# Split products read and written from the last column to the first, and two pads in the second attention's memory

## The chip, the cores and the metric

The kernel runs on one core of a Trainium2 chip. The number that counts is the time of the whole program on the device, in microseconds. The engines are named as in the profile: PE is TensorE's matmul side, PEld its loading of weights, DVE is VectorE, ACT ScalarE, POOL GpSimd, SP the engine that issues the DMAs.

## What is computed

Two layers on 16 sequences of 64 tokens with 512 features each (1024 tokens), all in float32. `ctx` has the same shape as `x`.

```python
x = x + L0_xattn(layernorm(x), ctx)      # 32 query heads, 8 key heads, head size 128, rope, mask
x = x + L0_ffn(layernorm(x))             # silu(gate) * up, cut to whole numbers, 512 -> 1376 -> 512
x = x + L1_xattn(layernorm(x), ctx)      # keys and values from ctx and x joined, q and k rms-normalised
x = x + L1_ffn(layernorm(x))             # two 512 x 512 layers, fake int8 quantisation, gelu between them
```

Each attention projects queries (512 to 4096), keys and values (512 to 1024 each), and its output (4096 to 512). These projections, and the gate and up products of the first feed-forward, need more precision than one pass of TensorE's fast float32 form (`F32R`) has.

## The kernel before

**Split products.** Every operand of a projection is kept as two tiles, `hi` (the value rounded to `F32R`) and `lo` (what the rounding left). `split_product` (L63) makes from each pair of blocks three matmuls: hi by hi, lo by hi, hi by lo, and adds all of them up in one bank of PSUM. Its `lhs` is the stationary operand (the weights of the array, 128 x 128), its `rhs` the moving one. Each of the three has its own stationary block, so each matmul comes with its own weight load (PEld). All matmuls at L70 of the profile are those of `split_product`.

**Where it is called.** In `attention` three parts call it. `kv_job` holds a block of 128 tokens (`kv_hi`, `kv_lo`) still and streams 2 x 128 columns of the key and value weights. `q_job` holds 128 columns of the query weights still and streams 512 tokens of `kv_hi`, `kv_lo`. `project` holds 128 tokens of the attention's result (`o_hi`, `o_lo`) still and streams 512 columns of the output weights. In `int_ffn` the gate and up products hold 128 weight columns still and stream 512 tokens. The down product of `int_ffn` (L1774) is a loop of its own: 128 tokens of `hid` held still, `down_hi` and then `down_lo` streamed, 512 columns each.

**Order on PE.** The program of PE is written out by hand: in each of the 32 units of an attention it issues the scores of one unit, fills in with the projections of others (`filling`), turns the probabilities and weighs the values, and DVE, ACT and POOL take results out of PSUM, split them and prepare what comes next behind semaphores. Four PSUM banks (`proj`) rotate under the projections.

**Where the tiles lie.** Tiles are placed one behind the other in a partition's memory, from the left in the order of their allocation, or from the right for those with `side="right"`. Nearly all large tiles are a whole number of 512 bytes per partition, so two of them have the same rest by 512 bytes unless small tiles lie between them. In the first attention and the first feed-forward nothing small lies between `kv0_hi` and `kv0_lo`, the weights, and `o_hi` and `o_lo` or `hid`: all have one rest. In the second attention the weights `att1_w_hi` and `att1_w_lo` have that rest too, then come the small tiles of the last feed-forward (3 x 32, 64, 4 x 32 and 3 x 64 bytes, 480 in all), and then `q_cols`, `k_cols`, `v_rows`, `k_rows`, `o_hi`, `o_lo` and the rest, 32 bytes short of it. `kv1_hi` and `kv1_lo` are placed from the right end, at a rest 64 bytes short of that of the weights. The tiles of the last feed-forward later lie on the memory of `kv1`.

Of the kernel before, what the change touches and what calls it, by code (L numbers as in the profile page):

```python
# [5 lines left out]
F32 = mybir.dt.float32  # L6
# [7 lines left out]
P = 128  # L14
# [46 lines left out]
    pass  # L61


def split_product(eng, out, terms, first=True, last=True):


    n = 0
    for lhs_hi, lhs_lo, rhs_hi, rhs_lo in terms:
        for a, b in ((lhs_hi, rhs_hi), (lhs_lo, rhs_hi), (lhs_hi, rhs_lo)):
            ins = eng.matmul(out, a, b, start=(first and n == 0), stop=(last and n == 3 * len(terms) - 1))  # L70
            n += 1
    return ins

# [417 lines left out]
def attention(nc, st, tag, rope, weights, source=None, following=None, tail=None):  # L491
# [45 lines left out]
    for u in range(UNITS):  # L537
        g, n = divmod(u, 4)
# [24 lines left out]
    with ExitStack() as ctx:  # L563
        def sb(name, shape, dt=F32):
            return ctx.enter_context(nc.sbuf_tensor(f"{tag}_{name}", shape, dt))

        def sem(name):
            return st.sem(f"{tag}_{name}")

        q_cols = sb("q_cols", [P, 4, NBH, 2, S])  # L570
        k_cols = sb("k_cols", [P, NB * KL])
        v_rows = sb("v_rows", [P, NB * KL // P, HD])
# [993 lines left out]
def int_ffn(nc, st, tag, weights, following):  # L1566
# [3 lines left out]
    with ExitStack() as ctx:  # L1570
        def sb(name, shape, dt=F32):
            return ctx.enter_context(nc.sbuf_tensor(f"{tag}_{name}", shape, dt))

        hid = sb("hid", [P, CF, TOK], F32R)
# [26 lines left out]
        def x_cols(tile, k, h):  # L1601
            return tile[:, k, BANK * h:BANK * (h + 1)]

        def out_bank(t):

            return banks[(t + 4) % 8]

        def width(c):
            return P if c < WIDE else REST
# [17 lines left out]
        @block.sync  # L1627
        def _(eng):
            def load_next(c, m):
                for i in range(3):  # L1630
                    split.need(eng, c, i + 1)
                    weights.load(eng, i, c + 1, m)

            load_ctx(eng, st, st.spare, 0)
            following.load(eng, 3)
            with eng.Fori(0, WIDE - 1) as c:
                load_next(c, P)
            load_next(WIDE - 1, REST)
            split.need(eng, 0, 3 * CF)
            for n in range(3):  # L1640
                following.load(eng, n)
# [105 lines left out]
        @block.tensor  # L1747
        def _(eng):
            pair_full.start(eng)

            def body(c, sub, m, m_next):
                split.need(eng, c, 2)
                for h in range(HALF):
                    if isinstance(c, int) and c == 0 and h == 1:
                        for t in range(4, NT):
                            intake.turn(eng, t)
                        eng.wait_ge(intake.x_split, 4)
                    pair_drained.need(eng, c, h + 1 - PAIRS)
                    for i in range(2):
                        last = split_product(eng, banks[4 * sub + 2 * h + i][:m], [  # L1760
                            (gu_hi[:, sub, i, k, 0:m], gu_lo[:, sub, i, k, 0:m],
                             x_cols(x_hi, k, h), x_cols(x_lo, k, h))
                            for k in range(KT)])
                    last.then_inc(pair_full.sem, 1)

            chunk_passes(eng, body)
            split.need(eng, 0, 3 * CF)
            for t in range(NT):
                if t % (NT // HALF) == 0:
                    clipped.need(eng, 0, CF * HALF - 1 + t // (NT // HALF))  # L1770
                for c in range(CF):
                    m = width(c)
                    for i, down in enumerate((down_hi, down_lo)):
                        last = eng.matmul(out_bank(t)[:], hid[:m, c, t * P:(t + 1) * P], down[:m, c, :],  # L1774
                                          start=(c == 0 and i == 0), stop=(c == CF - 1 and i == 1))
                last.then_inc(out_full, 1)

# [4 lines left out]
def build(nc, a, out):  # L1782
    st = State()
    with ExitStack() as ctx:
        st.sem = lambda name: ctx.enter_context(nc.semaphore(name))

        def sb(name, shape, dt=F32):
            return ctx.enter_context(nc.sbuf_tensor(name, shape, dt))
# [13 lines left out]
        def columns_scope(tag, n, side="left"):  # L1802

            scope = ExitStack()
            st.kv_hi, st.kv_lo = (scope.enter_context(nc.sbuf_tensor(f"{tag}_{part}", [P, KT, n], F32R, side=side))
                                  for part in ("hi", "lo"))
            return scope

        first = AttentionWeights(st, "att0", a["wq0"], a["wk0"], a["wv0"], a["wo0"])
# [12 lines left out]
                int_ffn(nc, st, "ffn0", inner, second)  # L1822
        with ExitStack() as scope:
            second.place(nc, scope)
            columns_scope("kv1", 2 * TOK, side="right").close()
            ffn = QuantFfn(nc, st, scope, "ffn1", a["gamma"], a["beta"], a["w1"], a["b1"], a["w3"], a["b3"], out)
            attention(nc, st, "att1", False, second, tail=ffn)
# [42 lines left out]
```

## Time and profile before

| | us |
|---|---|
| median of 3 runs | 1535.55 |
| lowest, highest | 1535.22, 1535.87 |
| span of the profiled execution | 1536.3 |

The profiled execution is one run of the program; its span goes from the first instruction to the last. An engine's busy time is the time in which at least one of its instructions is open. Matmuls are pipelined: the duration of one is longer than the distance from its start to the start of the next, so a rate is read from start to start and not from durations. A row of the timeline gives the start of a group of equal instructions that follow each other, the time from the first one's start to the last one's end, and after `x` how many they are.

### The profile page before, as it was taken

The numbers are of one execution on the slowest core, as the hardware profiler recorded it, in microseconds if no ns is written. First come the engines' busy times: TensorE is split into PE (matmuls) and PEld (weight loads), VectorE is DVE, ScalarE is ACT, GpSimd is POOL, SyncE is SP. The second block draws the span as 40 slices with busy tenths as digits, with TensorE's granted clock in tenths as the row PEclk, the third lists the DMA queues.
The fourth block names the chain that finished last, engine by engine and source line by source line (L and its number), as shares of the span: only waits on it lengthen the run. The fifth ranks groups of instructions, "written<-read, shape, count | busy, mean of one in ns | idle before, by whom it ended". The sixth has DMA issues, their size and how long they took to land.

```text
span 1536.3 us, 28681 instructions
## 1 busy us (share of the span) xinstructions
PE 1481.3 (96%) x11533; PEld 1273.9 (83%) x11536; DVE 950.8 (62%) x1983; ACT 599.3 (39%) x1434; POOL 564.6 (37%) x468
## 2 busy tenths in 40 slices
PE   6899999999999998999899999999999999999985
PEld 5788888888888877887788899888889989888973
DVE  7656666665666575666866455555645645565588
ACT  4313222221222234442355354444435444443556
POOL 4535354443535414561233132222312222231248
PEclk9999999999999999999899999999999999999999
DMA  6101021111102003220112011011101111010201
GB/s 197 42 28 53 19 68 29 42 38 33 48 22 70 21 6 98 75 57 21 48 30 62 1 42 29 28 43 28 42 1 42 29 29 42 21 50 1 83 2 55
DMA packets 84302, 64.45 MB, mean 42 GB/s; under 512 B 7280, under 2 KB 71024, under 8 KB 84176
## 3 DMA queue, kind: packets, MB, share of 16 engines
q1 hardware_dynamic: 83600, 62.47, 14.1%
q8 instruction: 91, 1.49, 0.4%
q14 instruction: 35, 0.29, 0.1%
q10 hardware_dynamic: 576, 0.20, 0.1%
HBM read 60.56 MB, written 2.10 MB: 41 GB/s over the span
## 4 chain that ended last, share of the span: by engine, by line
PE 47%; DVE 2%; POOL 1%; issue 1%; ACT 0%; DVEq 0%; ACTq 0%; POOLq 0%
PE att_proj L70 35%; PE att_att L798 4%; PE att_sco L756 4%; PE att_att L773 2%; PE att_proj L720 1%; PE att_sco L735 1%; POOL ffn_y L476 0%; DVE ffn_top L428 0%; DVE ffn_y L470 0%; POOL x_rows L414 0%; DVE ffn_y L424 0%; PE att_att L242 0%; DVE stats L383 0%; DVE x_rows L1051 0%; ACT ffn_y L435 0%
## 5 line engine op out<-in xcount | busy, mean ns | idle before, releaser
L148 POOL TENSOR_TENSOR att_w_lo<-w_raw,att_w_hi 128x512 fp32r<-128x512 f32 x160 | 207.0, 1319 | 183.3 <-ACT att_w_hi L143 175.8
L1414 POOL TENSOR_TENSOR att_probs<-att_probs,att_total 128x512 f32<-128x512 f32 x64 | 82.9, 1295 | 458.5 <-DVE att_total L1035 344.5
L70 PE MATMUL att_proj<-att_w_hi,kv_hi 128*128 128x256 f32 x768 | 221.7, 289 | 9.7 <-DVE kv_lo L260 9.7
L70 PE MATMUL att_proj<-att_w_hi,kv_lo 128*128 128x256 f32 x768 | 216.5, 282 | 0.0
L70 PE MATMUL att_proj<-att_w_lo,kv_hi 128*128 128x256 f32 x768 | 216.4, 282 | 0.0
L70 PE MATMUL att_proj<-kv_hi,att_w_hi 128*128 128x512 f32 x512 | 208.7, 408 | 1.5 <-DVE kv_lo L251 1.5
L70 PE MATMUL att_proj<-att_w_hi,att_o_hi 128*128 128x512 f32 x512 | 207.0, 404 | 1.9 <-issue 1.9
L70 PE MATMUL att_proj<-kv_lo,att_w_hi 128*128 128x512 f32 x512 | 202.7, 396 | 0.0
L70 PE MATMUL att_proj<-kv_hi,att_w_lo 128*128 128x512 f32 x512 | 202.6, 396 | 0.0
L70 PE MATMUL att_proj<-att_w_lo,att_o_hi 128*128 128x512 f32 x512 | 201.5, 394 | 0.0
L1051 DVE TENSOR_TENSOR x_rows<-att_proj,x_rows 128x512 f32<-128x512 f32 x128 | 88.4, 691 | 182.4 <-PE att_proj L70 182.3
L70 PE MATMUL att_proj<-att_w_hi,att_o_lo 128*128 128x512 f32 x512 | 201.2, 393 | 0.0
L1261 ACT ACTIVATE att_probs_t<-att_att 128x512 f32<-128x512 f32 x96 | 54.1, 598 | 364.5 <-PE att_att L773 364.5
L70 PEld LDWEIGHTS att_proj<-att_w_hi,kv_hi 128*128 128x128 f32 x768 | 146.4, 191 | 12.0 <-issue 9.6
L70 PEld LDWEIGHTS att_proj<-att_w_lo,kv_hi 128*128 128x128 f32 x768 | 146.5, 191 | 0.0
L70 PEld LDWEIGHTS att_proj<-att_w_hi,kv_lo 128*128 128x128 f32 x768 | 146.4, 191 | 0.0
L1251 ACT ACTIVATE att_probs<-att_sco,att_low,att_q_rms 128x128 f32<-128x128 f32 x256 | 113.9, 464 | 57.2 <-DVE att_low L1015 57.2
L1400 POOL TENSOR_TENSOR att_q_cols<-spare 128x512 f32<-128x512 f32 x64 | 85.8, 1341 | 121.5 <-DVE spare L966 121.5
L70 PE MATMUL ffn_bank<-kv_hi,kv_lo 128*128 128x512 f32 (+1 forms) x528 | 121.8, 393 | 6.3 <-DVE kv_hi L251 4.6
L70 PEld LDWEIGHTS ffn_bank<-kv_hi,kv_lo 128*128 128x128 f32 (+1 forms) x528 | 98.7, 187 | 29.1 <-DVE kv_hi L251 4.9
L70 PEld LDWEIGHTS att_proj<-kv_lo,att_w_hi 128*128 128x128 f32 x512 | 97.1, 190 | 22.7
L70 PEld LDWEIGHTS att_proj<-att_w_hi,att_o_hi 128*128 128x128 f32 x512 | 96.4, 188 | 23.0 <-issue 2.1
(167 smaller groups left out, 2743.6 us busy)
## 6 DMA issues: line engine op xcount, KB each, us to landing
w_raw<-in_wq SPq DMA_DIRECT2D x64, 256.0 KB, 2.9
w_raw<-in_wo SPq DMA_DIRECT2D x64, 256.0 KB, 2.8
w_raw<-in_wk SPq DMA_DIRECT2D x16, 256.0 KB, 3.0
w_raw<-in_wv SPq DMA_DIRECT2D x16, 256.0 KB, 3.5
w_raw<-in_gate_t SPq DMA_DIRECT2D x10, 256.0 KB, 2.9
w_raw<-in_up_t SPq DMA_DIRECT2D x10, 256.0 KB, 3.2
w_raw<-in_down_t SPq DMA_DIRECT2D x10, 256.0 KB, 3.0
spare<-in_ctx_t SPq DMA_DIRECT2D x4, 512.0 KB, 5.2
```

The costliest lines, as they stand in the source:

```text
L70: ins = eng.matmul(out, a, b, start=(first and n == 0), stop=(last and n == 3 * len(terms) - 1))
L148: eng.tensor_tensor(self.lo[:, chunk], self.raw[:, n % RAW_SLOTS], raw(self.hi[:, chunk]), ALU.subtract)\
L720: last = eng.matmul(proj[job % 4][rows, b:b + 1], squares[:, u % 2, b, g, part], st.ones[:, 0:1], start=True, stop=True)
L735: last = eng.transpose(bank[:, c * P:(c + 1) * P], k_rows[:, 4 * i + c], st.ident[:])
L756: last = eng.matmul(sco[job % 2][:, cols], q_cols[:, u % 4, b, :, :], k_cols[:, key], start=True, stop=True)
L773: last = eng.transpose(bank[:, c * P:(c + 1) * P], flat[:, (4 * i + c) * P:(4 * i + c + 1) * P], st.ident[:])
L798: last = eng.matmul(att_bank("out", u, i)[:, cols], v_rows[:, NBH * h + 4 * i + c], probs_t[:, i, cols], start=True, stop=True)
L1051: eng.tensor_tensor(st.x[:, row], proj[job % 4][:], st.x[:, row], ALU.add).then_inc(proj_drained, 1)
L1251: ins = eng.activation(probs[:, u % 2, b], sco[(u * SJ + i) % 2][:, c * KL:(c + 1) * KL], ACT.Exp, bias=low[:, u % 2, one], scale=q_rms[:, ...
L1261: eng.activation(probs_t[:, slot], att_bank("turn", u, i)[:], ACT.Copy).then_inc(turned_copied, 1)
L1400: eng.tensor_tensor(dst, a, b, ALU.add).then_inc(rotated, 1)
L1414: eng.tensor_tensor(probs[:, u % 2, 0:n], probs[:, u % 2, 0:n], total[:, u % 2, 0:n].unsqueeze(2).broadcast_to([P, n, KL]), ALU.mult)\
```

## The change

`backward` reverses the order in which an access pattern goes through its free dimensions; the numbers it names stay the same. `split_product` and the down product apply it to the output and to the moving operand, so column 511 (or 255) is read and written first and column 0 last, and each result still lands at its old address. The stationary operand is named as before. Two tiles that nobody uses are added in the second attention: 32 bytes ahead of `q_cols`, and 448 bytes at the right end ahead of `kv1_hi`. With them all large tiles of the second attention, and those of the last feed-forward at the right end, have the rest by 512 bytes that the weights have.

```diff
+def backward(ap):
+
+    return ap[:, ::-1] if len(ap.shape) == 2 else ap[:, ::-1, ::-1]
+
+
 def split_product(eng, out, terms, first=True, last=True):
-
 
     n = 0
     for lhs_hi, lhs_lo, rhs_hi, rhs_lo in terms:
         for a, b in ((lhs_hi, rhs_hi), (lhs_lo, rhs_hi), (lhs_hi, rhs_lo)):
-            ins = eng.matmul(out, a, b, start=(first and n == 0), stop=(last and n == 3 * len(terms) - 1))
+            ins = eng.matmul(backward(out), a, backward(b), start=(first and n == 0),
+                             stop=(last and n == 3 * len(terms) - 1))
             n += 1
     return ins
 
@@ -567,6 +572,8 @@
         def sem(name):
             return st.sem(f"{tag}_{name}")
 
+        if not rope:
+            sb("pad", [P, 8])
         q_cols = sb("q_cols", [P, 4, NBH, 2, S])
         k_cols = sb("k_cols", [P, NB * KL])
         v_rows = sb("v_rows", [P, NB * KL // P, HD])
@@ -1771,7 +1778,7 @@
                 for c in range(CF):
                     m = width(c)
                     for i, down in enumerate((down_hi, down_lo)):
-                        last = eng.matmul(out_bank(t)[:], hid[:m, c, t * P:(t + 1) * P], down[:m, c, :],
+                        last = eng.matmul(backward(out_bank(t)[:]), hid[:m, c, t * P:(t + 1) * P], backward(down[:m, c, :]),
                                           start=(c == 0 and i == 0), stop=(c == CF - 1 and i == 1))
                 last.then_inc(out_full, 1)
 
@@ -1822,6 +1829,7 @@
                 int_ffn(nc, st, "ffn0", inner, second)
         with ExitStack() as scope:
             second.place(nc, scope)
+            scope.enter_context(nc.sbuf_tensor("kv1_pad", [P, 112], F32, side="right"))
             columns_scope("kv1", 2 * TOK, side="right").close()
             ffn = QuantFfn(nc, st, scope, "ffn1", a["gamma"], a["beta"], a["w1"], a["b1"], a["w3"], a["b3"], out)
             attention(nc, st, "att1", False, second, tail=ffn)
```

## Rows read from the trace of the kernel before

**Rows 1.** Page, part 1: busy us, share of the span and instructions by engine.

```profile
PE 1481.3 (96%) x11533; PEld 1273.9 (83%) x11536; DVE 950.8 (62%) x1983; ACT 599.3 (39%) x1434; POOL 564.6 (37%) x468
```

**Rows 2.** Page, part 4: the chain that ended last, by engine and line.

```profile
PE 47%; DVE 2%; POOL 1%; issue 1%; ACT 0%; DVEq 0%; ACTq 0%; POOLq 0%
```

**Rows 3.** Stages: length; PE, PEld, DVE, ACT, POOL busy; granted clock; DMA share; GB/s.

```profile
0.00:574.00 574.00, 553.60 (x4080) 470.89 (x4080) 371.78 (x657) 158.12 (x287) 255.95 (x223) 0.99 0.17 48
574.00:748.00 174.00, 165.94 (x720) 134.57 (x720) 110.69 (x190) 68.62 (x121) 68.28 (x53) 0.98 0.21 57
...
757.00:1450.00 693.00, 692.91 (x6308) 618.54 (x6307) 392.37 (x972) 318.59 (x912) 184.69 (x146) 1.00 0.11 30
```

**Rows 4.** Groups by line and form, two of nine like these: count, busy us, mean ns.

```profile
L70 PE MATMUL att_proj<-att_w_hi,kv_hi 128*128 128x256 f32 x768 | 221.7, 289 | 9.7 <-DVE kv_lo L260 9.7
...
L70 PE MATMUL att_proj<-kv_hi,att_w_hi 128*128 128x512 f32 x512 | 208.7, 408 | 1.5 <-DVE kv_lo L251 1.5
```

**Rows 5.** Timeline of PE, first attention, output products: first and last of 22.

```profile
310.21 0.39 PE L70 MATMUL att_proj<-att_w_lo,att_o_hi 128*128 128x512 f32 x1
...
314.97 0.39 PE L70 MATMUL att_proj<-att_w_lo,att_o_hi 128*128 128x512 f32 x1
```

**Rows 6.** Timeline of PE, first attention, query products: first and last of 12.

```profile
298.22 0.40 PE L70 MATMUL att_proj<-kv_hi,att_w_hi 128*128 128x512 f32 x1
...
300.74 0.39 PE L70 MATMUL att_proj<-kv_lo,att_w_hi 128*128 128x512 f32 x1
```

**Rows 7.** Timeline of PE, feed-forward: 57 gate and up products; down products, first and last of 38.

```profile
639.51 13.08 PE L70 MATMUL ffn_bank<-kv_hi,kv_lo 128*128 128x512 f32 x57
...
714.62 0.39 PE L1774 MATMUL ffn_bank<-ffn_down_hi,ffn_hid 128*128 128x512 f32 x1
...
723.12 0.40 PE L1774 MATMUL ffn_bank<-ffn_down_lo,ffn_hid 128*128 128x512 f32 x1
```

**Rows 8.** Timeline of PE, second attention: outputs, 1st and 23rd; queries, 1st and 12th.

```profile
1007.22 0.40 PE L70 MATMUL att_proj<-att_w_hi,att_o_lo 128*128 128x512 f32 x1
...
1012.36 0.40 PE L70 MATMUL att_proj<-att_w_lo,att_o_hi 128*128 128x512 f32 x1
1012.59 0.39 PE L70 MATMUL att_proj<-kv_hi,att_w_hi 128*128 128x512 f32 x1
...
1015.16 0.39 PE L70 MATMUL att_proj<-kv_lo,att_w_hi 128*128 128x512 f32 x1
```

**Rows 9.** Timeline of PE, keys and values: first attention, 1st and 43rd; second, 1st and 69th.

```profile
293.06 0.28 PE L70 MATMUL att_proj<-att_w_lo,kv_hi 128*128 128x256 f32 x1
...
298.10 0.28 PE L70 MATMUL att_proj<-att_w_lo,kv_hi 128*128 128x256 f32 x1
...
1026.64 0.28 PE L70 MATMUL att_proj<-att_w_hi,kv_hi 128*128 128x256 f32 x1
...
1034.65 0.28 PE L70 MATMUL att_proj<-att_w_lo,kv_hi 128*128 128x256 f32 x1
```

**Rows 10.** Timeline of PE: groups of bf16 products with 512 columns, and eight transposes.

```profile
1520.87 0.81 PE L461 MATMUL att_proj<-ffn_w_t,ffn_x_t 128*128 128x512 bf16 x3
...
1528.98 1.24 PE L461 MATMUL att_proj<-ffn_w_t,ffn_x_t 128*128 128x512 bf16 x5
...
1462.70 1.04 PE L773 MATMUL att_att<-ident,att_probs 128*128 128x128 f32 x8
```

**Rows 11.** Timeline of all engines near 310.4 us: a matmul, and the next one's weight load.

```profile
310.44 0.39 PE L70 MATMUL att_proj<-att_w_hi,att_o_hi 128*128 128x512 f32 x1
310.44 0.19 PEld L70 LDWEIGHTS att_proj<-att_w_hi,att_o_lo 128*128 128x128 f32 x1
```

**Rows 12.** Timeline of PE: split products, 1st and 7th; that stretch's windows row (columns as above).

```profile
1470.69 0.63 PE L70 MATMUL att_proj<-att_w_hi,att_o_lo 128*128 128x512 f32 x1
...
1473.25 0.62 PE L70 MATMUL att_proj<-att_w_hi,att_o_lo 128*128 128x512 f32 x1
...
1470.50:1473.60 3.10, 3.10 (x8) 2.42 (x8) 2.92 (x10) 0.00 (x0) 2.00 (x3) 0.50 0.03 5
```

## The prediction

> **What bounds the kernel now.** Begin with the busy times: PE is busy 96% of the span, DVE 62%, ACT and POOL under 40% [rows 1]. The chain that ended last is mostly PE too [rows 2]. Then the stages: in the second attention PE is busy for 692.91 of 693 us, in the first for 553.6 of 574, in the feed-forward for 165.9 of 174, and the next busiest engine, DVE, needs 392, 372 and 111 us there; the granted clock is 0.98 to 1.00, the upper level of 2.4 GHz [rows 3]. So what a product costs on PE goes into the time nearly one for one, and no engine is near to taking over.
>
> A busy PE is not PE at its peak, so read its rate next, from start to start. Split products with 512 moving columns (six groups of 512 in the attentions, 528 gate and up products, 176 down) and with 256 (three groups of 768) are 3776 and 2304 in number [rows 4]. The distance between them:
> - first attention, outputs: 314.97 - 310.21 over 21 steps, 0.2267 us [rows 5]; queries: 2.52 over 11, 0.2291 [rows 6]
> - feed-forward, gate and up: (13.08 - 0.39) over 56, 0.2266; down: 8.50 over 37, 0.2297 [rows 7]
> - second attention, outputs: 5.14 over 22, 0.2336; queries: 2.57 over 11, 0.2336 [rows 8]
> - keys and values: 5.04 over 42, 0.1200 in the first attention, 8.01 over 68, 0.1178 in the second [rows 9].
>
> Against that, bf16 products with 512 columns stand (1.24 - 0.81) over 2, 0.215 us apart, and eight transposes (1.04 - 0.27) over 7, 0.110 [rows 10]. The second number is the pace at which 128-column weight loads can follow each other. Every split product is thus 8 to 19 ns over what PE does elsewhere in this trace. At the lower clock level (granted 0.50) the same products stand 2.56 over 6, 0.4267 apart, less than twice 0.215: there the excess is gone [rows 12].
>
> **What the excess is.** Same instruction, same shape, same engine, yet the output products take 0.2267 where weights and `o_hi` have one rest by 512 bytes, and 0.2336 where the rests differ by 32 bytes [rows 5, 8]. Keys and values go the other way, 0.1200 with one rest and 0.1178 with two [rows 9]. So time depends on where the two operands lie: what I read from it is that a product's moving operand and the next product's weight load get into each other's way in memory. The two start within the same hundredth of a microsecond [rows 11]. A product reads 2048 bytes in 0.215 us, four turns of 512; a weight load reads 512 bytes in 0.110 us, one turn. If they collide whenever they are at the same place of a turn, and run in opposite senses, they meet 2 + 1 = 3 times in the 0.110 us that both read; in the same sense 2 - 1 = 1 time, and from the same start that one meeting falls on the very end. The excess of 11.7 ns (0.2267 - 0.215) would be 3.9 ns a meeting. No row shows in which sense weights are read; that they go from the last column to the first is an assumption of the forecast. The Trainium skill (TensorE: Matmul & The Clock Gate, section Weight-path perf modes) says of another mode that its first 128 weight columns are loaded reversed, and gives the chunks of the fast weight load a negative step; no run here shows it for float32.
>
> **Reversing the products.** It adds and removes no instruction, no wait and no byte, and the order on every queue stays. What is to be had, with 0.215 and 0.110 as floors, is number times excess:
> - outputs, first attention: 768 x 11.7 ns = 9.0 us; queries 768 x 14.1 = 10.8
> - gate and up: 528 x 11.6 = 6.1; down 176 x 14.7 = 2.6
> - second attention: outputs 768 x 18.6 = 14.3; queries 768 x 18.6 = 14.3
> - keys and values: 768 x 10.0 = 7.7 and 1536 x 7.8 = 12.0
>
> In all 76.8 us. That is the upper bound. What stays is between 0 and one meeting of 3.9 ns; I take 3 ns, near one meeting, since the two reads start together only to within a hundredth of a microsecond and a product that is a few columns ahead catches up just before the load ends. 6080 x 3 ns = 18.2 us. The gain is 76.8 - 18.2 = 58.6 us. The lower bound of the edit is a loss, and is priced below. It also reverses the order of writing into PSUM; no row shows a backward write, so its price lies between nothing and the half-pace case below, and I take nothing, as every product writes the same 2048 bytes of the same bank.
>
> **The pads.** They cost no time of any engine: 32 and 448 bytes of memory, nothing fills or reads them. They bring every pair of operands in the second attention to one rest, on which the sum above relies. By themselves, with products still forward, they would turn the second attention's rates into those of the first: outputs 768 x 6.9 ns = 5.3 us less, queries 768 x 4.5 = 3.5 less, keys and values 1536 x 2.2 = 3.4 more, 5.4 us less in all. The other matmuls there keep the rest between their own operands except the transposes against `ident`, which already run at 0.110.
>
> **What is late next.** If the second attention gets some 40 us shorter, PE has about 650 us of work against 392 on DVE; in the feed-forward about 158 against 111 [rows 3]. The waits of the others for PE shorten with it. The start and the last feed-forward have few split products and don't change.
>
> **The sum.** 1536.3 - 58.6 = 1477.7 us for an execution like the profiled one. Its span is 0.75 us above the median of 1535.55, so the median goes to 1477.
>
> **Rivals.**
> 1. *Direction does nothing, rests do.* The excess is there in both senses, and only the pads act: 1535.55 - 5.4 = 1530 us. For it: every observed difference is between rests, none between senses. Against it: meetings that depend on the place should depend on the sense. Between this and the forecast lies a partial gain.
> 2. *Nothing changes.* The excess belongs to the weight load as such, and rests that seem to matter are neighbours in the program. 1535.5 us. The Trainium skill holds this (TensorE: Matmul & The Clock Gate, section Part 2, on LDWEIGHTS: loading the next weights takes no read bandwidth from the running matmul; SBUF — State Buffer, section SBUF: two separate sides: PE never waits on anyone there). The trace disagrees: 0.2267 and 0.2336 for one form [rows 5, 8].
> 3. *The product is held behind the weight load.* In the same sense a single meeting can last. If the weight load has the lead when they start, the product can't pass and goes at the load's pace for 0.110 us: 128 columns instead of 256, so 128 columns late, 0.215 / 4 = 54 ns. 6080 x 54 ns = 328 us, less the 76.8 of present excess: 1535.55 + 251 = 1787 us. It decides on who is first inside the hundredth of a microsecond of [rows 11]: if the product is, it pulls away.
> 4. *A descending stream runs at half pace*, in reading or in writing PSUM, at about the distance seen at the low clock: 3776 x (0.427 - 0.230) + 2304 x (0.213 - 0.118) = 744 + 219 = 963 us more, about 2500. The Trainium skill (SBUF — State Buffer, the box on cachelines) says that a non-contiguous PSUM pattern slows matmuls much; whether descending counts as that no run here shows, and neighbours stay neighbours.
>
> **How the numbers follow.** Forecast, between the whole 76.8 and about half of it, 1458 to 1500 us: 0.60. Rival 1 and the partial gains above 1500: 0.20. Rival 2: 0.08. Rival 3: 0.07. Rival 4: 0.05. The number is the forecast's, 1477. The range takes in the first two, 1458 to 1531, and leaves out 0.20. A measurement of this kernel tells about 0.2% from no change, 3 us, so rival 1 still counts as faster: faster 0.80, within 0.2% 0.08, slower 0.12.
>
> **What would show it.** In the timeline of the changed kernel the output products of both attentions should stand 0.215 to 0.219 us apart, and keys and values 0.110 to 0.114, with no difference left between first and second attention. The counts, the stages outside the split products and the granted clock stay. If outputs stand 0.2267 apart in both, it is rival 1; if 0.27, rival 3; if 0.43 at a granted clock of 1.00, rival 4. The forecast is wrong in its root if weights are read from the first column to the last: then the present sense is already the good one, and reversal adds meetings.

## The result and the profile after

| | before | after |
|---|---|---|
| median, us | 1535.71 (4 runs) | 1548.84 (4 runs, 1545.52 to 1550.14) |
| span of the profiled execution | 1536.3 | 1548.2 |
| PE busy | 1481.3 | 1493.6 |

The changed kernel is slower: its ratio is 1.0082, with a 95% interval of 1.007 to 1.0094. The forecast was a gain of 58.6 us; a loss of 13 us was measured, on the other side of no change and outside the range. The page of the changed kernel, part 1, answers [rows 1]:

```profile
span 1548.2 us, 28684 instructions
PE 1493.6 (96%) x11536; PEld 1274.9 (82%) x11536; DVE 949.0 (61%) x1983; ACT 597.2 (39%) x1434; POOL 561.2 (36%) x468
```

Busy time rose on PE by 12.3 us and the span by 11.9; PEld gained 1.0, and the other three lost 2 to 3 each. The windows of the stages (columns as in [rows 3]) say where:

```profile
0.00:574.00 574.00, 554.32 (x4051) 466.22 (x4052) 365.07 (x648) 155.43 (x283) 254.35 (x223) 0.99 0.17 48
574.00:748.00 174.00, 166.29 (x714) 131.99 (x713) 109.23 (x184) 68.30 (x121) 67.60 (x53) 0.98 0.21 57
757.00:1450.00 693.00, 686.54 (x6241) 612.12 (x6242) 390.20 (x955) 317.52 (x911) 183.26 (x145) 0.99 0.11 32
```

PE is as busy as before and gets through fewer matmuls in the same 574 us: 4051 against 4080. The stage ends later, and the later stages start later; that the third window is a little less full comes from that shift, since the pause between the stages now lies in it (from 775 to 1450 PE is busy for 674.84 of 675 us, where it was 674.91). The granted clock is the same: 0.99 and 0.98 in the first two windows, and 1.00 from 775 on in both kernels. So the rate of the products has changed, and it is read from start to start, as in [rows 5 to 9]. The timeline of PE in the first attention, output products (1st and 21st of 21) and query products (1st and 12th of 12):

```profile
301.86 0.40 PE L74 MATMUL att_proj<-kv_hi,att_w_hi 128*128 128x512 f32 x1
...
304.43 0.40 PE L74 MATMUL att_proj<-kv_lo,att_w_hi 128*128 128x512 f32 x1
...
311.19 0.40 PE L74 MATMUL att_proj<-att_w_lo,att_o_hi 128*128 128x512 f32 x1
...
315.85 0.40 PE L74 MATMUL att_proj<-att_w_hi,att_o_lo 128*128 128x512 f32 x1
```

Outputs stand 4.66 over 20, 0.2330 us apart, where they were 0.2267 [rows 5]; queries 2.57 over 11, 0.2336, where they were 0.2291 [rows 6]. In the feed-forward, 87 gate and up products; then the second attention, outputs (1st and 27th) and keys and values (1st and 20th):

```profile
639.72 20.46 PE L74 MATMUL ffn_bank<-kv_hi,kv_lo 128*128 128x512 f32 x87
...
1017.14 0.40 PE L74 MATMUL att_proj<-att_w_hi,att_o_hi 128*128 128x512 f32 x1
...
1023.21 0.40 PE L74 MATMUL att_proj<-att_w_lo,att_o_hi 128*128 128x512 f32 x1
...
1033.73 0.28 PE L74 MATMUL att_proj<-att_w_lo,kv_hi 128*128 128x256 f32 x1
...
1035.98 0.28 PE L74 MATMUL att_proj<-att_w_hi,kv_hi 128*128 128x256 f32 x1
```

Gate and up: (20.46 - 0.40) over 86, 0.2333 (0.2266 in [rows 7]). Outputs: 6.07 over 26, 0.2335, as before [rows 8]. Keys and values: 2.25 over 19, 0.1184 (0.1178 in [rows 9]). In this kernel a backward product of 512 columns goes at one pace, about 0.2334, which is the slow pace of the kernel before; nothing came near 0.215.

The mean distance in nanoseconds over all pairs of neighbours in an unbroken stretch, by kind of product, for the two kernels and the variants of the next section:

| | keys/values, att 0 | queries | outputs | gate/up | down | keys/values, att 1 | queries | outputs |
|---|---|---|---|---|---|---|---|---|
| before | 119.7 | 229.7 | 227.6 | 227.1 | 229.5 | 117.6 | 233.0 | 233.0 |
| after | 118.4 | 233.6 | 233.4 | 233.3 | 233.9 | 118.3 | 233.8 | 233.5 |
| direction alone | 118.4 | 233.6 | 233.4 | 233.4 | 233.9 | 119.9 | 233.6 | 233.4 |
| pads alone | 119.6 | 229.8 | 227.6 | 227.0 | 229.2 | 119.9 | 228.2 | 227.5 |

Number times difference accounts for the loss: outputs of the first attention 768 x 5.8 ns = 4.5 us, queries 768 x 3.9 = 3.0, gate and up 528 x 6.2 = 3.3, down 176 x 4.4 = 0.8, outputs and queries of the second attention 768 x 1.3 = 1.0, keys and values 768 x 1.3 = 1.0 less in the first and 1536 x 0.7 = 1.1 more in the second. In all 12.7 us, against 11.9 in the spans.

### The profile page after: what moved, and what is told of

The parts are those of the page before. It is cut to its first block, busy times and chain, and to the rows that moved or that the text cites. A ratio compares the mean times of both kernels' runs of the same rounds, so it can differ in the third digit from the quotient of the medians.

```text
span 1548.2 us, 28684 instructions
## 1 busy us (share of the span) xinstructions
PE 1493.6 (96%) x11536; PEld 1274.9 (82%) x11536; DVE 949.0 (61%) x1983; ACT 597.2 (39%) x1434; POOL 561.2 (36%) x468
## 4 chain that ended last, share of the span: by engine, by line
PE 46%; DVE 3%; POOL 1%; issue 1%; ACT 0%; DVEq 0%; ACTq 0%; POOLq 0%
PE att_proj L74 34%; PE att_att L805 4%; PE att_sco L763 4%; PE att_att L780 2%; PE att_proj L727 1%; PE att_sco L742 1%; POOL ffn_y L481 0%; DVE ffn_top L433 0%; DVE ffn_y L475 0%; POOL x_rows L419 0%; DVE att_probs_t L232 0%; DVE ffn_y L429 0%; DVE stats L388 0%; DVE kv_lo L265 0%; PE att_att L247 0%
## 5 line engine op out<-in xcount | busy, mean ns | idle before, releaser
L74 PEld LDWEIGHTS att_proj<-att_w_hi,kv_hi 128*128 128x128 f32 x768 | 146.1, 190 | 13.2 <-issue 11.0
L74 PE MATMUL ffn_bank<-kv_hi,kv_lo 128*128 128x512 f32 (+1 forms) x528 | 126.1, 403 | 5.9 <-DVE kv_hi L256 4.1
```

The lines of the kernel that those rows point to most:

```text
L74: ins = eng.matmul(backward(out), a, backward(b), start=(first and n == 0), stop=(last and n == 3 * len(terms) - 1))
```

## Experiments in the whole kernel

**Direction alone.** The changed kernel without its pads.

```diff
-        if not rope:
-            sb("pad", [P, 8])
...
-            scope.enter_context(nc.sbuf_tensor("kv1_pad", [P, 112], F32, side="right"))
```

> The changed kernel without its two pads: products go from the last column to the first, the second attention's tiles keep the rests of before. After the change a product with 512 columns stands 0.2335 us from the next in every stage, where it was 0.227 to 0.230 in the first attention and the feed-forward and 0.233 in the second attention. Theory A (the reversal itself costs 6 ns a product wherever the rests were alike, and the pads do nothing for backward products): 1548 us, and 0.2335 in the second attention too. Theory B (backward products want unlike rests, and the pads spoil that): the second attention comes nearer to 0.215 and the whole is under 1535 us.

Measured: 1549.88 us against 1536.44 (ratio 1.0086, 1.0072 to 1.01). So the direction is the loss, all of it. With backward products the pads matter in one kind only, keys and values of the second attention, 119.9 without and 118.3 with: 1536 x 1.6 ns = 2.5 us, 2.0 between the profiled spans (1550.2 and 1548.2).

**Pads alone.** The kernel before with the two pads.

```diff
+        if not rope:
+            sb("pad", [P, 8])
...
+            scope.enter_context(nc.sbuf_tensor("kv1_pad", [P, 112], F32, side="right"))
```

> The kernel before with the two pads and nothing else: forward products, all rests alike. If forward products with one rest are the good case wherever they stand, the second attention's output products go from 0.2336 to 0.227, its queries to 0.229, its keys and values from 0.1178 to 0.120, and the time is 5 us shorter, 1530 us. If neighbours in the program and not the rests make the difference, 1535.5 us.

Measured: 1532.69 us against 1536.44, ratio 0.9975 (0.9966 to 0.9985), 3.8 us less. The timeline of PE in the second attention, outputs (1st and 22nd), then keys and values (1st and 22nd):

```profile
1006.05 0.39 PE L70 MATMUL att_proj<-att_w_lo,att_o_hi 128*128 128x512 f32 x1
...
1010.81 0.39 PE L70 MATMUL att_proj<-att_w_lo,att_o_hi 128*128 128x512 f32 x1
...
1024.89 0.28 PE L70 MATMUL att_proj<-att_w_lo,kv_hi 128*128 128x256 f32 x1
...
1027.40 0.28 PE L70 MATMUL att_proj<-att_w_lo,kv_hi 128*128 128x256 f32 x1
```

Outputs 4.76 over 21, 0.2267, against 0.2336 [rows 8]; keys and values 2.51 over 21, 0.1195, against 0.1178 [rows 9]. So the rest counts for forward products, with opposite signs here for 512 and for 256 columns. By the table the terms are 768 x 5.5 = 4.2 and 768 x 4.8 = 3.7 less, 1536 x 2.3 = 3.5 more: 4.4 us less, which is also the difference between the profiled spans (1536.3 and 1531.9).

**Which of the two reversals.** Each of these two kernels has one of them alone, in `split_product` and in the down product, so the results land mirrored in their rows:

```diff
-            ins = eng.matmul(backward(out), a, backward(b), ...
+            ins = eng.matmul(out, a, backward(b), ...            # moving operand alone
+            ins = eng.matmul(backward(out), a, b, ...            # output alone
```

> The changed kernel with the moving operand alone backward; the output is written forward, so the results land mirrored in their rows. The parts run gave 0.2334 for this at every rest. If reading is what costs: the same as the changed kernel, 1548 to 1549 us.

> The changed kernel with the output alone written backward, the moving operand read forward; the results land mirrored. The parts run gave 0.2277 for this at rest 0. If writing into PSUM backward costs nothing: the time of the pads alone, 1533 us.

Moving operand alone: 1549.77 us against 1536.05, ratio 1.0093 (1.0078 to 1.0108), with the rates of the changed kernel. Output alone: 1532.83, ratio 0.9977 (0.9968 to 0.9987), with the rates of pads alone. The first and the 21st output product of the first attention, output alone:

```profile
311.22 0.39 PE L74 MATMUL att_proj<-att_w_hi,att_o_hi 128*128 128x512 f32 x1
...
315.75 0.39 PE L74 MATMUL att_proj<-att_w_lo,att_o_hi 128*128 128x512 f32 x1
```

They are 4.53 over 20, 0.2265 apart. Writing PSUM from the last column to the first costs nothing; reading the moving operand that way is the whole price.

## Experiments on the product by itself

These kernels leave out the computation and issue blocks of 48 products on PE alone, 12 after each other into each of four PSUM banks. Unless said otherwise, each product has another stationary block than the one before, and the loops have the form

```python
for k in range(48):
    eng.matmul(o(k), still[:, 128*(k%32) : +128], moved[:, 512*(k%8) + d : +512], ...)   # [:, ::-1] for back
```

where 4 d is the rest, the bytes by which the moving operand lies past the stationary one by 256. A row holds a whole block, so the distance is (length - length of one) over 47, and one is 0.39 to 0.40 us long (0.28 with 256 columns, 0.38 with bf16). Each such run was made once. The first products of a block sometimes go at another pace, so a mean over 48 can stand 1 ns off the steady one.

**All rests, both directions.**

> Leaves out the whole computation: TensorE alone runs runs of 48 products of 128x128 by 512 columns in float32r, each with a stationary block of its own, one run for each distance of 0, 32, ... 480 bytes between the rests of moving and stationary operand, forward and backward; the other engines are idle. If moving operand and weight load meet in memory, the distance from start to start depends on the rest: forward, 0.227 at 0 and 0.233 at 32 and at 448; backward, somewhere in the scan it falls to 0.215 to 0.219. If the excess belongs to the weight load as such, it is 0.226 or more at every rest and in both directions.

The timeline of PE: forward at rests 0, 32, 64 and 256, back at 0 and 256.

```profile
44.10 11.04 PE L68 MATMUL bank<-moved,still 128*128 128x512 f32 x48
54.98 11.37 PE L70 MATMUL bank<-moved,still 128*128 128x512 f32 x48
66.19 11.16 PE L72 MATMUL bank<-moved,still 128*128 128x512 f32 x48
...
133.22 11.05 PE L84 MATMUL bank<-moved,still 128*128 128x512 f32 x48
...
222.34 11.37 PE L100 MATMUL bank<-moved,still 128*128 128x512 f32 x48
...
311.95 11.36 PE L116 MATMUL bank<-moved,still 128*128 128x512 f32 x48
```

Forward, rest 0 and rest 256 give (11.04 - 0.39) / 47 = 0.2266, rests 64 and 320 give 0.2291, all others 0.2331 to 0.2341. The pattern repeats after 256 bytes, not 512. Backward, all 16 rests give 0.2333 to 0.2335. The rates of both whole kernels are found again here without any other engine at work.

**The parts of it.**

> Leaves out the whole computation, as the scan of rests; runs of 48 products that tell apart what the reversal is made of: the moving operand alone backward, the output alone backward, 256 columns in both directions, rests in steps of 4 bytes, 128 columns, one and the same stationary block for all, and bf16. If reading is what costs, the moving operand alone backward takes 0.2335 at rest 0 and the output alone 0.227; if writing is, the other way round. If the weight load is the partner, bf16 products show 0.215 in both directions. 256 columns: 0.120 forward at rest 0, 0.118 backward.

Moving operand alone back (rest 0), output alone back (rest 0), 256 columns forward at 0 and at 192, 256 columns back at 0, and bf16 back:

```profile
43.85 11.37 PE L68 MATMUL bank<-moved,still 128*128 128x512 f32 x48
...
133.47 11.09 PE L84 MATMUL bank<-moved,still 128*128 128x512 f32 x48
...
222.02 5.91 PE L100 MATMUL bank<-moved,still 128*128 128x256 f32 x48
...
239.12 5.63 PE L106 MATMUL bank<-moved,still 128*128 128x256 f32 x48
...
267.16 5.84 PE L116 MATMUL bank<-moved,still 128*128 128x256 f32 x48
...
513.66 10.52 PE L170 MATMUL bank<-moved_b,still_b 128*128 128x512 bf16 x48
```

The moving operand is the slow part (0.2334) and the output is not: the block's mean is 0.2277, but only its first products are slower, and its second half stands at 0.2266, the forward pace. With 256 columns forward is 0.1198 at rest 0, the rest that all keys and values of the first attention have, and 0.1138 at 192; backward is 0.1183 at rest 0. Plain bf16 has no such excess in either direction: 0.2158 forward once steady, 0.2158 back. The same run has rests from 4 to 28 bytes, and there backward isn't one pace: the means are 0.2334 and 0.2336 at rests 28 and 16, 0.2355 to 0.2367 at 4, 8, 20 and 24, and 0.2399 at 12.

**Does the excess follow the weight load?** This is the test of the forecast's main step. If the products meet the loads, a stationary block of 32 columns, a quarter of the bytes, must show a quarter of the meetings.

> Leaves out the whole computation, as the scan of rests; runs of 48 float32r products. The stationary block has 128, 96, 64 or 32 columns, so that its load is shorter and the product of 512 columns is not. If the excess over 0.2155 is made of meetings of the product's reading with the next weight load (11 ns forward and 18 ns backward at rest 0 with 128), it shrinks with the block: at 32 columns to about a quarter, 3 and 4 ns. If it is a fixed price of float32r or of the direction, it stays at 11 and 18 whatever the block. Moving both operands on by the same bytes changes nothing if only the distance between them matters. Products of 384, 320 and 192 columns: the excess is that of 512, since the load is over in 0.11 us.

Stationary block of 128 columns, forward and back, then of 32 columns, forward and back, all at rest 0; then 128 columns forward with both operands moved on by 16 and by 32 bytes:

```profile
44.01 11.04 PE L68 MATMUL bank<-moved,still 128*128 128x512 f32 x48
...
88.45 11.36 PE L76 MATMUL bank<-moved,still 128*128 128x512 f32 x48
...
311.75 11.29 PE L116 MATMUL bank<-moved,still 128*32 128x512 f32 x48
...
356.25 11.36 PE L124 MATMUL bank<-moved,still 128*32 128x512 f32 x48
...
411.98 11.21 PE L134 MATMUL bank<-moved,still 128*128 128x512 f32 x48
...
423.03 11.09 PE L136 MATMUL bank<-moved,still 128*128 128x512 f32 x48
```

With 32 columns the forward excess is larger ((11.29 - 0.39) / 47 = 0.2319 against 0.2266), and backward the distance is 0.2334 with 128, 96, 64 and 32 columns alike. The loads did get shorter, from 188 to 109 ns in the mean. So the excess isn't a number of meetings that shrinks with the load. The stationary block still has some part in it forward, since its width changed the pace by 5 ns; what part, no run shows.

Moving both operands on by the same bytes keeps the distance between them. By 32, 64 and so on up to 224 bytes it changed nothing (0.2266 in the second half of each block), so what counts isn't the place of the moving operand by itself. But by 16, 48 and so on up to 240 bytes all eight blocks stood at 0.230. So the distance between the two isn't all that counts either, unless it is what the block before did, since blocks of both kinds ran in turn.

384 columns took 0.1734 forward and 0.1778 back at rest 0, 320 columns 0.147 at every rest and in both directions, 192 columns 0.111 to 0.112 likewise. At 192 columns that is about the 0.110 of the transposes [rows 10], so there the weight load is likely what sets the pace. With 320 columns the same loads follow each other at 0.147, so they don't set it, and direction and rest have dropped out all the same.

**What does the excess need?**

> Leaves out the whole computation, as the other runs of 48. Is the excess one of the number form or of the bytes that are read? bf16 with a step of 2 in the moving operand covers 2048 bytes per 512 columns as float32r does: theory of the bytes, its 0.2158 rises and depends on rest and sense; theory of the form, it stays 0.2158. float32r that reads one and the same column 512 times: theory of the bytes, no excess (0.2155) and no difference of senses; theory of the form, 0.2267 or more. Columns of 224 to 496: all distances so far settle near a whole multiple of 6.67 ns (113.3, 120, 226.7, 233.3, 240), 8 cycles of 1.2 GHz; if that is a grain, the distance goes in such steps and not with every 16 columns.

First bf16 with every second column read, so that 512 columns span 2048 bytes, forward and back (47 of 48 records); then float32 with one column read 512 times, output back (with the output forward only the first product was slower); then eight columns read 64 times:

```profile
44.16 10.78 PE L90 MATMUL bank<-moved_b,still_b 128*128 128x512 bf16 x47
54.78 11.26 PE L92 MATMUL bank<-moved_b,still_b 128*128 128x512 bf16 x47
...
229.76 10.52 PE L124 MATMUL bank<-moved,still 128*128 128x512 f32 x48
...
272.81 10.53 PE L132 MATMUL bank<-moved,still 128*128 128x512 f32 x48
```

Spread over 2048 bytes, bf16 has the excess too: (10.78 - 0.39) / 46 = 0.2259 forward, where the record that is missing is at an end of the block, and (11.26 - 0.39) / 47 = 0.2313 backward, where it is inside. Float32 that reads the same one or eight columns again has none: (10.52 - 0.38) / 47 = 0.2157. So it isn't the format. Nor is it the length of the weight load: bf16 products of 128 columns stand 0.056 apart where float32 ones stand 0.111, so bf16 loads take at most half the time, and spread bf16 has the excess all the same. It goes with the new bytes that the moving operand spans per column: it is there with 4 a column (float32, or bf16 with every second column) and not with 2 (plain bf16) or with columns that repeat. A stationary block of one repeated column leaves it, 0.2317 forward and 0.2333 back. By length it is no price per column. As a yardstick take the columns over the 2.4 GHz of the upper clock level, which is 213.3 ns for 512 and 106.7 for 256: at rest 0, 512 columns are 13.3 above it forward and 20 back, 256 columns 13.1 and 11.7, 448 columns (186.7) 16 and 20, 320 columns (133.3) 13.3 both ways. I had expected whole steps of 6.67 ns; 226.7, 233.3 and 240 do stand on such steps, 202.7 with 448 columns doesn't.

**Rest in steps of 4 bytes.**

> Leaves out the whole computation, as the scan of rests; forward products with 512 and with 256 columns at every rest from 0 to 252 bytes in steps of 4. The scan by 32 repeats after 256 bytes. If the meetings have a grain of some bytes there are narrow good rests that the steps of 32 and 64 bytes missed; for 512 columns better than 0.2267, for 256 better than the 0.1139 at 192. If 0 and 192 are already the best, the whole gain that placement can give in this kernel is that of the query, output and feed-forward products at 0 and of keys and values at 192.

Forward, 512 columns at rest 0 and 256 columns at rests 0, 16, 112 and 192:

```profile
42.99 11.04 PE L68 MATMUL bank<-moved,still 128*128 128x512 f32 x48
...
761.19 5.91 PE L196 MATMUL bank<-moved,still 128*128 128x256 f32 x48
...
784.06 5.60 PE L204 MATMUL bank<-moved,still 128*128 128x256 f32 x48
...
921.13 5.64 PE L252 MATMUL bank<-moved,still 128*128 128x256 f32 x48
...
1035.84 5.62 PE L292 MATMUL bank<-moved,still 128*128 128x256 f32 x48
```

For 512 columns rest 0 is the best of 64 (0.2266); the worst, 20, 116 and 212, have 0.240. For 256 columns rest 0 is in the middle of the 64 (0.1198), 16, 112 and 192 are the best (0.1132 to 0.1140), and the worst, 4, has 0.1230. This points to a kernel with two rests. It also tells when the direction matters: forward is under 0.2330 at 28 of the 64 rests and near or above backward's 0.2333 at the other 36, so a product on a poor rest has little to lose by reversal. In the kernel before, those of the second attention had such a rest.

## From the findings to a faster kernel

**Keys and values at rest 192.** The kernel before with two pads (the one ahead of `kv1_hi` is 128 bytes here), and a gap of 64 bytes inside each weight tile behind the two chunks that hold key and value weights, the tile moved on so that these lie at 192 and the query and output weights at 0:

```diff
+class Chunks:
+    SHIFT = 16
...
+        self.head = tile[:, 0:n].rearrange("p (c n) -> p c n", n=BANK)
+        self.rest = tile[:, n + self.SHIFT:CHUNKS * BANK + self.SHIFT].rearrange("p (c n) -> p c n", n=BANK)
...
+        if ahead:
+            tile("w_ahead", ahead, F32)
```

> Forward products and the two pads, and in both attentions the key and value weights moved so that they lie 192 bytes (by 256) past the tokens they are multiplied with, while query, output and feed-forward products stay at a rest of 0. The fine scan gives 0.1137 us for 256 columns at 192 and 0.1200 at 0. Theory of the map (each product costs what the scan shows for its own rest and sense): 2304 products x 6.3 ns = 14.5 us off the 1532.7 of the pads alone, 1518 us, a ratio of 0.988 to the kernel before. If another engine or the queues behind the products hold it, less than half of that.

Measured: 1524.46 us against 1536.05, ratio 0.992 (0.9906 to 0.9935). It falls 6 us short of what was expected, and the rows name the place of most of it: keys and values of the first attention (1st and 45th), and two stretches of those of the second (22 and 70 products):

```profile
292.06 0.28 PE L70 MATMUL att_proj<-att_w_hi,kv_hi 128*128 128x256 f32 x1
...
297.25 0.28 PE L70 MATMUL att_proj<-att_w_lo,kv_hi 128*128 128x256 f32 x1
...
1017.02 0.28 PE L70 MATMUL att_proj<-att_w_lo,kv_hi 128*128 128x256 f32 x1
...
1019.41 0.28 PE L70 MATMUL att_proj<-att_w_lo,kv_hi 128*128 128x256 f32 x1
...
1020.59 0.28 PE L70 MATMUL att_proj<-att_w_lo,kv_hi 128*128 128x256 f32 x1
...
1028.72 0.28 PE L70 MATMUL att_proj<-att_w_lo,kv_hi 128*128 128x256 f32 x1
```

5.19 over 44, 0.1180; 2.39 over 21, 0.1138; 8.13 over 69, 0.1178. The same instructions on tiles with the same rests have two steady paces, even a microsecond apart. The mean over all was 117.7 in the first attention and 114.2 in the second. Against the 113.7 that was expected this is 768 x 4.0 = 3.1 us and 1536 x 0.5 = 0.8; where the other 2 to 3 us are isn't shown.

**Is it the place or the predecessor?** The tiles at the addresses of each attention, and then blocks of keys behind blocks of queries and the other way round.

> Leaves out the whole computation: key and query products alone, with the blocks, the order hi, lo, hi and the distances between tiles that the first and the second attention have, other engines idle, the weights moved on by 0 to 240 bytes in steps of 16. In the kernel with keys at 192 the second attention's keys and values stand 0.1142 us apart as the scan says, the first attention's 0.1177 instead of 0.1137. If the layout of the first attention makes that, it shows here too, 0.1177 at 192 in the first layout and 0.1137 in the second, and another rest may be better for it; if the work of the other engines makes it, both layouts show 0.1137 here. Queries: 0.2267 at 0 in both.

> Leaves out the whole computation: 48 key products behind 12 query products, and 48 query products behind 12 key products, in the first attention's layout, at rests from 0 to 240 in steps of 16, forward and backward, other engines idle. Theory: the distance of forward products at one rest has more than one steady value, and what ran before picks one; 0.1178 at 192 here against 0.1136 behind keys. Backward query products: 0.2333 at every rest here too, since no state was seen in which they differ.

Five blocks of 48 key products. The first three are from the kernel with the attentions' own addresses, at rest 192: behind key products, behind query products, and behind the block that ran behind query products, with all tiles 32 bytes on. The last two are from the kernel of predecessors, rests 112 and 192, both behind query products.

```profile
139.65 5.62 PE L97 MATMUL bank<-big 128*128 128x256 f32 x48
...
608.45 5.82 PE L201 MATMUL bank<-big 128*128 128x256 f32 x48
614.10 5.82 PE L203 MATMUL bank<-big 128*128 128x256 f32 x48
```

```profile
133.03 5.64 PE L103 MATMUL bank<-big 128*128 128x256 f32 x48
...
174.98 5.82 PE L123 MATMUL bank<-big 128*128 128x256 f32 x48
```

The layouts of the two attentions make no difference beyond the rest. What ran before does: (5.62 - 0.28) / 47 = 0.1136 behind keys and 0.1179 behind queries, at rest 192; the last row is rest 192 behind queries once more, 0.1179. The pace then persists: the third row and the six blocks after it, with the tiles up to 224 bytes on, are keys behind keys, and all stay at 0.1179. So it isn't the kind of the predecessor alone that decides. At rest 112 it is 0.1140 behind queries too. Query products have two paces as well: with the weights moved on by 16 bytes, 0.2267 in one kernel and 0.2334 in the other. Backward keys and values stood at 0.1177 to 0.1199, and backward queries at 0.2334, or 0.2367 at three rests: in these steps of 16 bytes the backward direction has no rest as good as the best forward ones.

**Keys and values at rest 112.** The kernel of rest 192 with other gaps (`LEAD = 4`, `SHIFT = 40`, 24 elements ahead, and 32 bytes ahead of `kv1_hi`).

> As the kernel with keys at 192, but the key and value weights lie 112 bytes (by 256) past the tokens. In the own-layouts run the same 48 key products at 192 took 0.1136 us when they followed other keys and 0.1178 when they followed queries; at 112 they took 0.1133 at once. If 112 holds the fast pace whatever comes before: 0.1133 in both attentions, 2304 x 6.6 ns = 15.2 us off the 1532.7 of the pads alone, 1517.5 us, ratio 0.988. If the pace hangs on what comes before at every rest, the first attention stays near 0.1177 and the time near the 1524.5 of the keys at 192.

Measured: 1519.32 us (1517.54 to 1522.3) against 1536.38, ratio 0.9881 (0.9865 to 0.9898), as expected. Keys and values of the first attention, 1st and 36th:

```profile
293.16 0.28 PE L70 MATMUL att_proj<-att_w_hi,kv_hi 128*128 128x256 f32 x1
...
297.13 0.28 PE L70 MATMUL att_proj<-att_w_lo,kv_hi 128*128 128x256 f32 x1
```

3.97 over 35, 0.1134; the means are 114.3 and 114.0. The terms: 768 x 5.4 = 4.1 us and 1536 x 3.6 = 5.5 from keys and values, and, taken from the pads alone, 4.2 and 3.7 from outputs and queries of the second attention, 17.5 in all; 17.1 were measured. This kernel is faster than both the kernel before and the changed one, with all products forward.

## Why the prediction was wrong, point by point

- **What bounds the kernel** held. 12.7 us on the products became 11.9 us of span, and in the best variant 17.5 became 17.1. Nothing else took over.
- **"What the excess is"** is the step that failed. It read the excess over 0.215 as three meetings between a moving operand and the next weight load, 3.9 ns each. The start in one hundredth of a microsecond [rows 11] and the dependence on rests were rows; the counting was an idea, and the 3.9 ns were fitted to one number of [rows 5] and tried on no second one. A load of a quarter of the bytes should have removed most of the excess; it removed none (0.2319 forward against 0.2266, and 0.2334 backward with either). That weights are read from the last column to the first was named as an assumption. No run shows their sense, and it no longer matters: without meetings the two senses have nothing to agree on.
- **"Reversing the products"** took that all but 3 ns would go. In its place 0.2333 to 0.2338 was measured for every kind with 512 columns, so the excess of the output products grew from 11.7 to 18 ns where it should have shrunk. That is the opposite of the forecast gain: 12.7 us more on the products in place of 58.6 less. The floor was wrong as well: 0.215 is the pace of bf16 products, whose moving operand spans half the bytes. No run with 512 different columns of float32 went below 0.2266. Keys and values are the one kind that came out as small gains, 768 x 1.3 = 1.0 us in the first attention where 5.4 was in the sum.
- **The two unknown costs inside it.** Writing PSUM backward was taken at nothing, and is nothing (ratio 0.9977 with it, 0.9975 without). The Trainium skill (SBUF — State Buffer, the box on cachelines) says that any non-contiguous PSUM pattern slows matmuls significantly; a descending one, if that counts as non-contiguous, doesn't in these runs. Reading backward was priced only inside the meetings and as the half pace of rival 4. The nearest rows gave a middle price: one form stood at 0.2267 or 0.2336 by its place [rows 5, 8]. A backward read that falls to the slow one of these two paces is 768 x 6.9 + 768 x 4.5 + 528 x 7 + 176 x 4 = 13.2 us for the products that had the fast one. That rival, a small loss from the rows' own two paces, was missing, and it is what happened. The chance of 0.12 for a slower kernel lay wholly on losses of 251 and 963 us.
- **The pads** were right in mechanism and sign: 5.3 and 3.5 less and 3.4 more were forecast, 4.2, 3.7 and 3.5 came, 3.8 us in the medians against 5.4. The term that was mis-sized is the outputs: the mean over all of them changed by 5.5 ns, not 6.9, because means are not the steady stretches of [rows 5, 8] (227.5 and 233.0, against 226.7 and 233.6). In the changed kernel that gain is lost, because backward products of 512 columns stood at 0.2333 to 0.2336 with either rest (direction alone and the changed kernel).
- **Rival 1** (direction does nothing, rests do) was right on rests and wrong on direction. **Rival 2**, by which nothing changes and rests are mere neighbours, fell: the kernel got slower, and the two pads alone, with every neighbour as before, moved the rates of the second attention. But it had a point: at one rest what ran before chose between 0.1136 and 0.1179. Its sentence from the Trainium skill (TensorE: Matmul & The Clock Gate, section Part 2, that loading the next weights takes no read bandwidth from the running matmul) fits the runs with smaller loads, whose excess is no smaller. **Rivals 3 and 4** were not seen: no stretch stood at 0.27, nor at 0.43 with a granted clock of 1.00.

Still open is why a float32 product of 512 columns takes 11 to 24 ns more than one of plain bf16, why the rest by 256 bytes and the direction choose between these values, and what puts the same products on one of two paces. The 64 rests and the lengths give the pattern, not the cause. One row narrows it: at a granted clock of 0.50 the same products stand 0.4267 apart [rows 12], which is 512 columns over 1.2 GHz, so the excess is there only at the upper clock level.

## What to carry to other kernels

A distance that changes with place says that there is something to gain, not in which direction; before a reversal of thousands of products is costed, a block of 48 of them alone, forward and back and at a few rests, gives its price. It gave the rates of 512 columns here to about a per cent; for keys and values at rest 192 it was over 3% too low in the first attention, where they went at the slower of their two paces. Where a floor comes from another format, ask whether its operand spans as many bytes per column. What was best in this kernel is float32 moving operands forward, with 512 columns at the rest of the stationary ones by 256 bytes and with 256 columns 112 bytes past it. In another kernel, read the rate again in the whole of it.

## What the runs showed of the hardware

- A float32 product of 512 columns, each with its own 128-column weight load, takes 0.2266 us at best forward and 0.2333 backward, and up to 0.240 in both directions at poor rests; of 256 columns 0.1132 and 0.1177 at best. bf16 takes 0.2158 either way, and loses that when its columns are spread over 2048 bytes (0.226 and 0.231). The Trainium skill (SBUF — State Buffer, section Specifications (TRN2), on cachelines) has each change of 16-byte line pay a penalty and wants at least two hits per line for full bandwidth. Repeated columns without excess fit that; float32 read in order has four hits per line and pays all the same, and that 256 and 512 columns had the same 13 ns forward at rest 0 doesn't look like a price per line.
- The rest between moving and stationary operand acts with a period of 256 bytes (seen in steps of 32), and forward a step of 4 bytes already changes the rate (0.2266 at 0, 0.2360 at 4). With the rest kept at 0, both operands moved on by 16 bytes gave 0.2300 in place of 0.2266.
- The same 48 products on the same tiles took 0.1136 or 0.1179 us each, by what had run before.
- Writing a PSUM bank from the last column to the first cost nothing (1532.83 us with it, 1532.69 without).
